# A graph-transformer layer on one core: first tile turned beside the weights, two places for rows, projections and turned tiles, edge work and scatter dealt anew

## What is computed

```python
xn = _layernorm(x, axis=-1)
x = x + _L0_gnn_ref(xn, edge_index, W, att_src, att_dst, bias) + _L0_mix_ref(xn[None], Wq, bq, Wk, bk, Wv, bv, Wo, bo)[0]
x = x + _L0_ffn_ref(_layernorm(x, axis=-1)[None], w1, b1, w2, b2)[0]
...
# mix: linear attention, 16 heads of 64
Q = elu(x @ Wq.T + bq) + 1;  K = elu(x @ Wk.T + bk) + 1;  V = x @ Wv.T + bv
KV = einsum("bphd,bphe->bhde", K, V);  Z = einsum("bphd,bhd->bph", Q, K.sum(axis=1))
out = (einsum("bphd,bhde->bphe", Q, KV) / (Z[..., None] + 1e-6)).reshape(B, P, D) @ Wo.T + bo
# gnn: graph attention, 4 heads of 256
xp = (x @ W).reshape(N, H, C);  e = leaky_relu(a_src[src] + a_dst[dst], 0.2)
ee = exp(e - segment_max(e, dst)[dst]);  alpha = ee / segment_sum(ee, dst)[dst]
out = relu(segment_sum(xp[src] * alpha[:, :, None], dst).reshape(N, H * C) + bias)
```

## Time and profile before

| | us |
|---|---|
| median of three runs | 3360.26 |
| the profiled execution: its time | 3363.04 |
| its span, first to last instruction | 3361.1 |
| TensorE busy | 3119.3 (93%) |
| VectorE busy | 2615.5 (78%) |
| ScalarE busy | 1227.4 (37%) |
| GpSimd busy | 1009.4 (30%) |
| mean granted TensorE clock | 0.973 |

### The profile page before, as it was taken

The page is one execution under the profiler, slowest core; times in us unless marked ns, Lnnn a source line. Parts: engine busy times, 40 slices in busy tenths (PEclk is TensorE's granted clock), DMA queues, the critical chain, the costliest instruction groups (busy, mean ns, idle before and its releaser), DMA issues. The chain is left out here.

```text
span 3361.1 us, 42506 instructions
## 1 busy us (share of the span) xinstructions
PE 3119.3 (93%) x14512; PEld 2540.1 (76%) x14512; DVE 2615.5 (78%) x4560; ACT 1227.4 (37%) x1596; POOL 1009.4 (30%) x698
## 2 busy tenths in 40 slices
PE   6899999996999999898979999999999999499997
PEld 5778888865888888676667888887887888377776
DVE  5577677765777777557889999999999976577784
ACT  2011111121111111212356565566556543366665
POOL 1246776756677667650000000000000000000000
PEclk8999999998999999999999999999999999699999
DMA  7943333343444444544544453454345221433331
GB/s 252 374 93 68 60 55 67 62 121 68 90 89 90 86 88 96 125 90 140 157 129 121 126 145 105 113 135 132 103 129 154 72 62 35 129 91 87 92 92 37
DMA packets 286038, 366.20 MB, mean 109 GB/s; under 512 B 190330, under 2 KB 190430, under 8 KB 285910
## 3 DMA queue, kind: packets, MB, share of 16 engines
q1 hardware_dynamic: 95828, 282.24, 28.7%
q0 software_dynamic: 184656, 65.68, 11.2%
q10 hardware_dynamic: 5426, 16.70, 1.4%
HBM read 272.64 MB, written 90.80 MB: 108 GB/s over the span
## 5 line engine op out<-in xcount | busy, mean ns | idle before, releaser
L1447 PE MATMUL G_acc<-values,whole_plain 125*125 125x257 f32 x5000 | 1108.2, 383 | 45.8 <-DVE whole_plain L1407 30.2
L1447 PEld LDWEIGHTS G_acc<-values,whole_plain 125*125 125x125 f32 x5000 | 939.2, 189 | 204.8 <-DVE whole_plain L1407 40.9
L357 POOL DMA_INDIRECT counts<-E_twins_now,E_cells_now x400 | 867.9, 2170 | 387.1 <-issue 248.0
L1311 ACT ACTIVATE whole_plain<-whole_plain,G_asrc_slope 125x750 f32<-125x750 f32 (+1 forms) x400 | 377.8, 946 | 418.7 <-DVE whole_plain L1394 417.9
L1394 DVE SCALAR_TENSOR_TENSOR whole_plain<-whole_plain,G_asrc_most 125x750 f32<-125x750 f32 (+1 forms) x400 | 411.1, 1028 | 46.3 <-PE G_acc L1447 45.0
L1285 POOL DMA_DIRECT2D gat<-xT_plain x100 | 53.6, 536 | 959.5 <-ACT xT_plain L1327 959.5
L978 DVE SCALAR_TENSOR_TENSOR N_least<-xT_plain,asrc_all,N_least 125x750 f32<-125x750 bf16 (+1 forms) x336 | 338.9, 1013 | 0.0
L254 PE MATMUL V_v_ps<-whole,xT_space 128*125 128x512 f32 x1200 | 293.6, 402 | 29.3 <-DVE xT_space L282 20.8
L254 PE MATMUL Q_q_ps<-whole,xT_space 128*125 128x512 f32 x1200 | 288.4, 399 | 20.8 <-DVE xT_space L282 20.8
L254 PEld LDWEIGHTS V_v_ps<-whole,xT_space 128*125 128x125 f32 x1200 | 221.3, 188 | 101.3 <-DVE xT_space L282 40.1
L254 PE MATMUL K_v_ps<-K_wv,xT_space 128*125 128x512 f32 x1200 | 292.7, 400 | 0.0
(11 more groups left out here) (177 smaller groups left out, 3308.3 us busy)
## 6 DMA issues: line engine op xcount, KB each, us to landing
whole_plain<-counts SPq DMA_DIRECT2D x222, 328.1 KB
counts<-K_zeros POOLq DMA_DIRECT2D x50, 763.5 KB, 8.3
xT_whole<-xnT SPq DMA_DIRECT2D x75, 500.0 KB, 3.6
whole_plain<-counts SPq DMA_DIRECT2D x74, 382.8 KB
xnT<-xT_whole SPq DMA_DIRECT2D x25, 500.0 KB, 8.2
gat<-xT_plain POOLq DMA_DIRECT2D x100, 125.0 KB, 2.4
E_row<-edge_keys ACTq DMA_DIRECT2D x25, 488.3 KB
E_row<-edge_keys SPq DMA_DIRECT2D x25, 488.3 KB
```

Of the source, the lines that this page charges most:

```text
L357: nc.gpsimd.indirect_dma_start(out=counts_cells, out_offset=bass.IndirectOffsetOnAxis(ap=self.cells_now[:, slot, c:c + 1], axis=0), in_=se ...
L1311: nc.scalar.activation(here, here, ACT.Exp, bias=asrc_slope[:, u % H, j:j + 1]).then_inc(exp_ready, 1)
L1447: m = nc.tensor.matmul(acc[0:T, t, 0:CW], weight[:, k % RING, t * T:(t + 1) * T], values[:, j, u % H, :], start=(j == 0), stop=(j == NT - 1))
```

## The change

- **First tile beside the weights.** The first tile of x is turned, copied and split after the fourth weight block in block 1 (before: at the start of block 2). The store of the keys is issued after the first five weight loads, the biases are loaded once their places in the ring are free and are waited for in block 2, and the arrays for the edges share space with the edge row.
- **Two places for rows of x** in block 2: the load of tile g+2 is issued when tile g is turned.
- **No edges in the first three tiles** (`SKIP = 3`): tile g prepares unit g-3. Block 2 prepares 22 units, block 3 two, block 4 all 25 tiles one each and one ahead of them. Before: 25, none, 25.
- **Two places for queries** in block 4: two query projections run ahead, then each tile is turn, query of the tile after next, mix.
- **Two places for turned tiles** in block 5 (`xT_whole`, `xT_other`).
- **Low parts on GpSimd** in block 5 from product 30 on (`LATE = NT + 5`); the wait for the whole scatter moves from product 25 to 30, and the 25 passes are spread over 17 products and not 22.
- **Batches dealt** 38, 2, 44 and 16.

```diff
-UNITS_K, UNITS_P, UNITS_Q = 20, 2, 23
+BATCHES_K, BATCHES_P, BATCHES_Q = 38, 2, 44
+SKIP, UNITS_K, UNITS_P = 3, 22, 2
...
-    rows = sb("rows", [T, D])
+    rows = sb("rows", [T, 2, D])
...
                 for tile, e in ((src_c, a["src"]), (dst_c, a["dst"])):
                     sp.dma_start(tile[:, :, :], e.rearrange("(b c p) -> c b p", b=CB, p=CH)).then_inc(edges_loaded, 16)
-                load_rows(sp, rows, a["x"][0:T, :], x_loaded)
-                weights.load(sp, blocks)
-                sp.wait_ge(weights.turned, len(blocks))
-                for tile, row in ((bk_row, a["bk"]), (bv_row, a["bv"])):
-                    sp.dma_start(tile[:, :], row.partition_broadcast(T)).then_inc(rows_loaded, 16)
+                load_rows(sp, rows[:, 0, :], a["x"][0:T, :], x_loaded[0])
+                weights.load(sp, range(weights.ring))
                 sp.wait_ge(keys_made, 1)
                 sp.dma_start(a["keys_dram"].rearrange("(b c p) -> c b p", b=CB, p=CH), key_c[:, :, :]).then_inc(keys_stored, 16)
-                sp.wait_ge(rows_loaded, 32)
+                weights.load(sp, range(weights.ring, len(blocks)))
+                for tile, row, n in ((bk_row, a["bk"], 12), (bv_row, a["bv"], 13)):
+                    sp.wait_ge(weights.turned, n)
+                    sp.dma_start(tile[:, :], row.partition_broadcast(T)).then_inc(rows_loaded, 16)
+                load_rows(sp, rows[:, 1, :], rows_of(a["x"], 1), x_loaded[1])
                 sp.wait_ge(keys_stored, 16)
...
-                weights.turn(pe, blocks)
+                weights.turn(pe, range(EARLY))
+                pe.wait_ge(xn_ready, 1)
+                turn_rows(nc, tr, rows[:, 0, :], ident, turned)
+                weights.turn(pe, range(EARLY, len(blocks)))
...
@@ K tiles, VectorE
-                if more:
-                    edges.prepare(dve, chain, g + 1)
+                if fixed(g, SKIP):
+                    edges.prepare(dve, chain, g - SKIP)
                 dve.wait_ge(kv_done, g + 1)
...
@@ weights of Q, VectorE
+                chain = Chain(dve, unit_link)
+                edges.prepare(dve, chain, UNITS_K)
                 weights.take_low(dve, range(KB))
+                edges.prepare(dve, chain, UNITS_K + 1)
...
@@ Q tiles, VectorE
-                if fixed(g, 0, NT - 2):
-                    edges.prepare(dve, chain, g + (NT + 1))
+                edges.prepare(dve, chain, g + FIRST)
...
@@ Q tiles, TensorE
-            query(0)
+            query(0, 0)
+            query(1, 1)
             def body(g, n):
-                if fixed(g, 1):
-                    mix(g - 1)
                 pe.wait_ge(q_scaled, g + 1)
                 turn_rows(nc, trq, q, ident, q_turned)
-                if fixed(g, 0, NT - 2):
+                if fixed(g, 0, NT - 3):
                     pe.wait_ge(qb_ready, g + 1)
-                    query(g + 1)
+                    query(g + 2, n)
+                mix(g)
...
@@ V products
-    TURN = NT + 23
+    TURN, LATE = NT + 23, NT + 5
...
-        done_by = [(NT * max(0, min(22, q + i - NT))) // 22 for i in range(2)]
+        done_by = [(NT * max(0, min(TURN - 1 - LATE, q + i - LATE))) // (TURN - 1 - LATE) for i in range(2)]
...
+                if q == LATE:
                     sp.wait_ge(edges.scattered, 16 * NCH)
...
+            for q in range(LATE, WHOLE - 1):
+                pool.wait_ge(xT_high, q + 1)
+                split_low(nc.gpsimd, q).then_inc(xT_low_late, 1)
...
-                if q + 1 < WHOLE:
-                    nxt = xT[:, (q + 1) % 2, :, :, :]
+                if q < LATE:
                     dve.wait_ge(xT_high, q + 1)
-                    low(nc, nxt[:, 1, :, :], xT_whole[:, :, :], nxt[:, 0, :, :]).then_inc(xT_low, 1)
+                    split_low(nc.vector, q).then_inc(xT_low, 1)
```

More of the change, by code:

```diff
@@ L352, in scatter_unit, with scatter_batch @@
         pool.sem_inc(self.seen, 1)
[L353 to L356 removed]
+        self.scatter_batch(pool, counts_cells, u, slot, 0)
+    def scatter_batch(self, pool, counts_cells, u, slot, batch):
+        nc = self.nc
+        if batch:
+            pool.wait_ge(self.scattered, u * (16 * CPU) + 16 * BATCH)
+            pool.sem_inc(self.seen, 1)
+        for c in range(batch * BATCH, (batch + 1) * BATCH):
             nc.gpsimd.indirect_dma_start(
@@ L444, in keys_and_values @@
         spare_i = psb("spare_i", [CH, BATCH], I32)
-        src_c, dst_c = psb("src_c", [CR, CB, CH], I32), psb("dst_c", [CR, CB, CH], I32)
-        key_c = psb("key_c", [CR, CB, CH])
+        src_c, dst_c = (edges.row[0:CR, i * CB * CH:(i + 1) * CB * CH].bitcast(I32).rearrange("p (b c) -> p b c", b=CB) for i in range(2))
+        key_c = edges.row[0:CR, 0:CB * CH].rearrange("p (b c) -> p b c", b=CB)
         ktr = pps("ktr", [128, 4, 128])
@@ L491, in _ @@
             def _(act):
-                weights.take_high(act, blocks)
+                weights.take_high(act, range(EARLY))
+                take(act, 0, 0)
+                weights.take_high(act, range(EARLY, len(blocks)))
                 act.wait_ge(zeros_set, 1)
@@ L591, in _ @@
             chain.step(nc.vector.memset(root[:, :], 0.0))
-            dve.wait_ge(xT_high, 1)
-            low(nc, xT[:, 0, 1, :, :], xT_whole[:, :, :], xT[:, 0, 0, :, :]).then_inc(xT_low, 1)
-            edges.prepare(dve, chain, 0)
+            dve.wait_ge(rows_loaded, 32)
             ahead_of_tiles(chain)
@@ L632, in _ @@
         def _(pe):
-            pe.wait_ge(xn_ready, 1)
-            turn_rows(nc, tr, rows, ident, turned)
             def body(g, n):
@@ L692, in _ @@
                 load_turned(sp, 0)
-                sp.wait_ge(weights.turned, 2 * KB)
-                for tile, row in ((bq_row, a["bq"]), (bo_row, a["bo"])):
-                    sp.dma_start(tile[:, :], row.partition_broadcast(T)).then_inc(rows_loaded, 16)
-                sp.wait_ge(rows_loaded, 32)
             @block.gpsimd
             def _(pool):
-                edges.scatter(pool, a["counts_cells"], UNITS_K, UNITS_K + UNITS_P)
+                edges.scatter(pool, a["counts_cells"], BATCHES_K, BATCHES_K + BATCHES_P)
             @block.scalar
             def _(act):
+                act.wait_ge(edges.cells_ready, UNITS_K + 1)
+                edges.load(act, a["keys_dram"], UNITS_K + 1)
                 weights.take_high(act, range(KB))
+                act.wait_ge(edges.cells_ready, UNITS_K + 2)
+                edges.load(act, a["keys_dram"], UNITS_K + 2)
                 for j in range(KB):
```

194 lines of the change are left out of this document (112 added, 82 removed).

## The result

The changed kernel takes 3374.8 us (median of 20 runs, 3353.6 to 3388.1); the kernel before, on the same chip, 3359.5 (20 runs, 3354.8 to 3368.5). The ratio is 1.0036, with a 95% interval of 1.0019 to 1.0054: 12 us slower by the ratio and 15 by the medians, where 35 us faster was forecast. Single runs now differ by 34 us, before by 14. The profiled execution is one of the short ones, 3356.7 us with a span of 3354.8.

The account below looks back on a forecast made before the run. TensorE, busy 93% of the span, was taken as the bound, so only its idle time and the clock lost behind it could return; seven terms summed to -35.3 us, from 3360.3 to 3325.0, range 3304 to 3345 (8 in 10).

Parts of the forecast that it names:

- the end of the Q tiles: Last Q tiles to first V product: VectorE's added units and last chain delay V's start, +10.2 us, bounds +4 and +14.
- start of the K tiles: Before the first K product: earlier key store and first tile, biases awaited later, first product at 45.3 against 58.0, -12.7 us.
- K tiles and their end: K tiles 0 to 4 (-23.7 us) and the end of the K tiles (+4.9 us) taken together.
- weights of Q: From kv_sum to first query: GpSimd drops out, two VectorE units come in, 53.9 us against 60.8, -7.0 us.
- V products: Product 31 waits for GpSimd until S + 194 (S: V's start); half hold-up cancels later gains, 0 us, -9 to +16.
- K tiles 0 to 4: First five K tiles: late edge rows and lower clock cost 25.7 us; all but 2.0 comes back, -23.7 us.
- end of the K tiles: Between the last half of V and kv_sum: a 6.2 us VectorE unit, mostly uncovered, +4.9 us, bounds +4 and +6.
- Start of the Q tiles: First queries: 8.66 us wait before the first turn goes, gaps of 2.4 and 1.4 appear, -7.0 us, bounds -10 and -3.
- GpSimd setting the end of a block: Any block: listed sign that the forecast is wrong, if GpSimd sets a block's end again; no size given.
- full hold-up: Rival, V products: GpSimd's subtraction and VectorE's steps take turns; V +16, sum -16, 3344 us; chance 0.17.
- my half: V products: GpSimd's 1.9 us subtraction holds VectorE's steps up for half its length, 0.95 us per product, 16 in all.
- The rival that went slower: Last 19 V products: GpSimd's subtraction sets the pace, gain gone from 6.2 us each, 3366 us at 6.5; chance 0.05.

Follow-up runs that it names:

- GpSimd out of the way: The changed kernel with batches dealt 39-4-40-17 instead of 38-2-44-16; 3368.9 us, ratio 1.0032.

## Why the prediction was wrong

Two terms failed: V, put at 0, for which the pace of GpSimd's scatter was taken too fast, and the end of the Q tiles, where SyncE's list was left out and GpSimd's batches had no term at all. Step by step, against the terms of the forecast sum, in the profiled executions:

```
                           forecast   measured
start of the K tiles        -12.7      -13.9
K tiles and their end       -18.8      -19.5
weights of Q                 -7.0       -3.3
Q tiles, start and end       +3.2      +11.8
V products                    0.0      +20.8
the rest                      0.0       -2.3
sum                         -35.3       -6.3
median over that run         -2.8      +18.1
```

- *Start of the K tiles, K tiles 0 to 4, end of the K tiles: right*, each within 1.2 us in the sum, and for the reasons given: no wait for an edge row, the first product 1.2 us earlier than 45.3. The parts of the change behind these terms were not tried one by one.
- *Weights of Q: right in sign, mis-sized by 3.7.* No wait for GpSimd before the first query. VectorE's last split ends 54.0 us into the block instead of 50.4. From the end of kv_sum to the first product with the mixer's blocks it is 27.0 us, 7.0 more than before, where I gave the first unit 4.9; from there to the last split it is 5.2 more, where I had 3.7. It was within the bounds.
- *Start of the Q tiles: right*; the gaps of 2.36 and 1.59 at the first queries were forecast as 2.4 and 1.4. The turn of tile 23 comes 561.5 us behind the first query instead of 556.3, with one query of 11.3 us more done by then: -6.0 for the -7.0 of the forecast.
- *End of the Q tiles: failed, +17.9 for +10.2.* I worked out VectorE's list and took TensorE, ScalarE and VectorE for all that is in the chain. SyncE's list was moved too: it waits for a unit before it stores the base row. That makes VectorE wait 8.55 and 4.03 us for x rows, 7.6 us in all (613.6 with GpSimd out of the way, 606.0 with the row stored first; my steps give 605.6). The forecast looked at SyncE only for the last store.
- *GpSimd in the Q tiles: not priced.* I took 44 batches for harmless, since there had been 46. But the 46 ran at 13.1 us each and so filled the 602.4 us of the stage to its end already; at 14.1 us 44 of them fill 620 us, at 14.7 more still. In three of four profiles of the changed kernel GpSimd sets V's start, and the stage is 9 to 23 us longer than in the first. That this is most of what the median has over the first profiled execution is inferred from these profiles. The forecast named GpSimd setting the end of a block as a sign of being wrong, but had no term and no chance for it here; why the pace grew stays open.
- *V products: the step that failed most.* The mechanism was right, product 31 waits for GpSimd's queue behind sixteen batches. I put it at S + 194 and called it even with the S + 192 of before. It came at S + 206.3. The last transfer, and the subtraction that product 31 waits for:

```profile
1558.49 2.00 POOL L362 DMA_INDIRECT counts<-E_twins_now,E_cells_now  x1 [0.30 <-issue]
1559.71 3.10 POOL L1104 TENSOR_TENSOR xT_space<-V_xT_other,xT_space 128x1000 fp32r<-128x1000 f32 x1
```

The pace of 12.07 is that of nine intervals before the change. Over the fifteen intervals of the changed kernel it was 12.90, which makes 12.4 us: the whole of the 12.3 by which product 31 is later than S + 194. (The forecast's S + 191.7 is the end of the last transfer's 2.3 us; the transfer starts at S + 201.9 and this end is at S + 204.2.) No run shows why the pace was slower; with the old kernel and sixteen batches in V it was 12.4. Behind product 31 came 138.0 us instead of 131.5. The hold-up is not in these 6.5 us, since with 13 batches it is as large and V takes 131.6 there. VectorE's first pass comes 9.7 us behind product 31's start, with 13 batches 7.8; the rest is open.
- *Hold-up.* The two-step pass takes 2.17 us alone. VectorE's passes and GpSimd's subtractions behind product 31:

```profile
1572.52 4.25 DVE L1010 SCALAR_TENSOR_TENSOR N_least<-whole_plain,asrc_all,N_least 125x875 f32<-125x875 bf16 x2
1578.89 6.30 DVE L1010 SCALAR_TENSOR_TENSOR N_least<-whole_plain,asrc_all,N_least 125x875 f32<-125x875 bf16 x4
```

```profile
1572.70 3.15 POOL L1104 TENSOR_TENSOR xT_space<-V_xT_other,xT_space 128x1000 fp32r<-128x1000 f32 x1 [1.72 <-ACT xT_space L279]
...
1594.21 2.34 POOL L1104 TENSOR_TENSOR xT_space<-xT_whole,xT_space 128x1000 fp32r<-128x1000 f32 x1 [6.79 <-ACT xT_space L279]
```

Two steps take 4.25, four 6.3 instead of 4.3: a step that meets a subtraction stands for 2 us more. With the low parts on VectorE no step of a pass took over 1.13 us; here ten of the 48 took 3.15 to 3.22. That is the full hold-up, to which I gave 0.17 as a rival, but only at about half of the nineteen subtractions, and the 48 steps together take 76.1 us instead of 54.0: 22 more, between the 16 of my half and the 32 of a full one. The exclusion that the Trainium skill states ("SBUF — State Buffer", "Who interferes with whom") agrees with these rows. The subtraction takes 2.34 to 3.27 us here, not 1.9; the Trainium skill's "GPSIMD Engine Reference", section 3.1, would have given an estimated 2.2. The sizes were off, the effect small: with 13 batches V is 1 to 2 us shorter than with the low parts on VectorE, where I had given this half as 0 with bounds of -9 and +16.
- The rival that went slower had the wrong mechanism: GpSimd's subtraction is far below 6.2 us. What took the gain back was the scatter, GpSimd's work that had been there all along, and the late x rows.

With the deal 39-4-44-13 and the base row stored first, the kernel takes 3323.4 and 3322.0. That this is near the forecast of 3325.0 is in part luck: in the first of its two profiles the start gives -14.5, the K tiles and their end -18.2, the weights of Q -1.9, the Q tiles +3.6, V -8.6 and the rest -2.2, in sum -41.8 for the -35.3 of the forecast. V, which the forecast left unchanged, makes up for the weights of Q. With sixteen batches the forecast had no gain in V; with 13 the two places for turned tiles bring product 31 to S + 182.8, from S + 192 before. It is the best version found, 37 to 39 us below the kernel before; with 14 batches in V it is the same within the measurement.

## What to carry over

When work is taken off one engine's path, add up the whole list of the engine that is next, here GpSimd's 100 batches stage by stage, at the slowest pace seen and not at that of its fastest stage (12.07 us in V, 13.1 in the Q tiles, before the change); an engine that fills every stage to its end has no slack to lend. A batch of background work may stand beside the main work up to the point where the first consumer asks for the last of it; past that point each one costs nearly its full length (11 to 12 us here), and a table of three or four deals finds the point. If code moves, write down the queue of every issuing engine around it, the one that only issues transfers too: a store behind a wait delays the load that needs its buffer.

## What was not expected of the hardware

- A store of 448 KB issued 0.3 us behind a load of 488 KB on the same queue was waited for 6.6 us on average, one that is issued by itself 2.3 to 2.4.
- GpSimd's four indirect transfers of 125 rows, with the wait for their landing, took 11.3 us at the least. On average they took 12.07 in V before the change, 12.7 to 13.1 in V after it, 13.7 to 14.7 in its Q tiles, and the same program differed by 1 us per batch from one execution to the next.
- A two-input subtraction of 128 x 1000 took 2.33 to 3.27 us on GpSimd against 1.19 on VectorE, and a two-input step of VectorE's that met it took 3.2 us instead of 1.12. On balance the move still gained 1 to 2 us.
- Behind its wait of 26.7 us TensorE took 7.64 us for a product that takes 5.85, at a mean granted clock of 0.68 over 1540 to 1582 us.
